# Whole float32 operands in place of split float32r ones in a two-layer transformer block

## What is computed

```
def layer1(x, Wq, Wk, Wv, Wo):                      # 16 heads of 128
    q, k, v = split_heads(x @ Wq), split_heads(x @ Wk), split_heads(x @ Wv)
    scores = einsum('bhsd,bhtd->bhst', q, k) * 128 ** -0.5 + mask   # 64-token blocks, |bi - bj| <= 2
    return merge_heads(einsum('bhst,bhtd->bhsd', softmax(scores), v)) @ Wo

def layer2(x, w_router, wq, bq, wk, bk, wv, bv, wo, w_gate, w_up, w_down, ln1_w, ln2_w):
    sel, sel_scores, pos = the 128 tokens of each batch with the highest x . w_router
    h = rms_norm(sel, ln1_w)
    q, k, v = rope(h @ wq + bq), rope(h @ wk + bk), h @ wv + bv     # 16, 8 and 8 heads of 128
    x1 = sel + merge(causal_attention(q, k, v)) @ wo                # all 256 rows one sequence
    h2 = rms_norm(x1, ln2_w)
    processed = x1 + (silu(h2 @ w_gate) * (h2 @ w_up)) @ w_down     # 2048 wide
    g = sigmoid(sel_scores)
    return x with the chosen rows set to g * processed + (1 - g) * sel

x = layernorm(x + layer1(x, ...))
x = layernorm(x + layer2(x, ...))
```

## Time and profile before

| | |
|---|---|
| runs | 1374.06, 1374.06, 1374.99 us; median 1374.06 |
| profiled execution | 1373.61 us, its span 1371.9 us |
| mean granted TensorE clock | 0.981 |
| busy: TensorE matmul / VectorE / ScalarE / GpSimd | 94% / 58% / 44% / 18% |
| HBM | 79.20 MB read, 8.91 MB written |

### The profile page before, as it was taken

How to read it: one execution, slowest core, us unless ns; L and a number is a source line. 1 busy time by engine, 2 the same in 40 slices (tenths; PEclk the granted TensorE clock), 3 DMA queues, 4 the chain that set the end, 5 groups by cost and what they waited for, 6 DMA issues and landing times.

```text
span 1371.9 us, 19013 instructions
## 1 busy us (share of the span) xinstructions
PE 1290.8 (94%) x7296; PEld 1097.2 (80%) x7296; DVE 791.8 (58%) x2219; ACT 605.3 (44%) x1422; POOL 247.6 (18%) x234
## 2 busy tenths in 40 slices
PE   6999999999999999988999999999999948999897
PEld 5888989898989898877798979898989834445696
DVE  4556565556565656566666756655565657542244
ACT  4544444454444444444454434354444433334353
POOL 2111111111111201023120212020211121000086
PEclk9999999999999999999999999999999979999898
DMA  5110100010111102022310101010101035555063
GB/s 167 41 32 16 47 30 33 32 32 31 32 32 47 62 1 77 1 100 70 123 47 16 47 27 47 16 47 16 47 16 46 24 137 188 192 194 169 0 192 131
DMA packets 62411, 89.34 MB, mean 65 GB/s; under 512 B 3232, under 2 KB 36000, under 8 KB 62320
## 3 DMA queue, kind: packets, MB, share of 16 engines
q1 hardware_dynamic: 61904, 86.81, 19.3%
q0 software_dynamic: 416, 1.31, 0.3%
HBM read 79.20 MB, written 8.91 MB: 64 GB/s over the span
## 4 chain that ended last, share of the span: by engine, by line
PE 75%; DVE 13%; ACT 6%; issue 2%; DMA 2%; POOL 2%; SPq 0%; ACTq 0%; POOLq 0%; DVEq 0%
PE proj L872 34%; PE y L872 11%; PE s L872 8%; PE o L872 8%; DVE arena L1343 6%; PE tp L951 4%; PE proj L880 3%; PE s L880 3%; ACT arena L1142 3%; ACT prob L1180 2%; DVE prob L1378 1%; PE o L880 1%; DVE bn_out L1442 1%; POOL arena L1651 1%; DVE yacc L1428 1%
## 5 line engine op out<-in xcount | busy, mean ns | idle before, releaser
L872 PE MATMUL proj<-arena 128*128 128x256 f32 (+1 forms) x3456 | 633.6, 333 | 8.5 <-DVE arena L1343 8.2
L872 PEld LDWEIGHTS proj<-arena 128*128 128x128 f32 x3456 | 531.2, 190 | 72.0 <-DVE arena L1343 13.1
L1180 ACT ACTIVATE prob<-prob,stat 128x384 f32<-128x384 f32 (+1 forms) x256 | 150.9, 590 | 488.7 <-DVE stat L1378 488.7
L1651 POOL TENSOR_TENSOR arena<-wraw,arena 128x1024 fp32r<-128x1024 f32 x75 | 182.1, 2438 | 861.7 <-ACT arena L1142 861.6
L1343 DVE TENSOR_TENSOR arena<-proj,arena 128x512 fp32r<-128x512 f32 (+1 forms) x266 | 148.0, 562 | 305.4 <-ACT arena L1142 304.3
L872 PE MATMUL s<-arena 128*128 128x384 f32 (+2 forms) x870 | 194.0, 336 | 11.1 <-DVE arena L1343 11.1
L872 PE MATMUL y<-arena 128*128 128x512 f32 x762 | 199.2, 397 | 0.5 <-DVE yacc L1428 0.5
L872 PE MATMUL o<-arena 128*128 128x256 f32 (+2 forms) x960 | 197.0, 325 | 0.7 <-DVE arena L1343 0.6
L1343 DVE TENSOR_TENSOR arena<-tp,arena 128x384 fp32r<-128x384 f32 (+2 forms) x257 | 133.6, 520 | 82.1 <-ACT arena L1142 81.8
L872 PEld LDWEIGHTS s<-arena 128*128 128x128 f32 x870 | 150.3, 189 | 29.9 <-DVE arena L1343 16.3
L1142 ACT ACTIVATE arena<-proj 128x512 fp32r<-128x512 f32 (+1 forms) x266 | 127.9, 488 | 95.1 <-PE proj L872 87.5
(11 more groups left out here) (151 smaller groups left out, 692.3 us busy)
## 6 DMA issues: line engine op xcount, KB each, us to landing
wraw<-in_L_attn_Wq SPq DMA_DIRECT2D x16, 512.0 KB, 3.4
wraw<-in_L_attn_Wk SPq DMA_DIRECT2D x16, 512.0 KB, 3.3
wraw<-in_L_attn_Wv SPq DMA_DIRECT2D x16, 512.0 KB, 3.3
wraw<-in_L_attn_Wo SPq DMA_DIRECT2D x16, 512.0 KB, 3.7
late<-in_L_ffn_wq SPq DMA_DIRECT2D x16, 512.0 KB, 4.9
late<-in_L_ffn_wo SPq DMA_DIRECT2D x16, 512.0 KB, 3.9
yacc<-in_L_attn_hidden_states SPq DMA_DIRECT2D x16, 256.0 KB, 3.0
y_dram<-yacc SPq DMA_DIRECT2D x16, 256.0 KB, 3.1
```

What stands on the lines that cost most here:

```text
L872: ins = e.matmul(out_ap, l[a], r[b], start=first and i == 0 and j == 0, stop=final and i == n - 1 and j == 2, skip_group_check=skip)
L1180: e.activation(prob[s][:, 0:n], prob[s][:, 0:n], ACT.Exp, bias=stat[:, 4 * s + 1:4 * s + 2], scale=-1.0, accum_out=stat[:, 4 * s + 2:4 * s ...
L1651: e.tensor_tensor(lo, wraw[n % RAW_SLOTS][:], hi.bitcast(F32), ALU.subtract).then_inc(*G_.inc("wsplit", n, "lo"))
```

## The change

All products take whole float32 operands, through one function. `hi_part`, `lo_part`, the weight splits, the raw places and `unit_row` go; ScalarE copies results out of PSUM once, and TensorE waits for that copy. The arena is one float32 tensor: both batches' turned x, q and k for two heads, v for two pairs of heads, four places for heads' outputs, and fifteen places for weights, through which all of `stream` passes, layer 2's attention weights included; a load is issued as its place is left. Batch 1's x is turned inside batch 0's heads (a tile every eighth unit), batch 0's by VectorE and ScalarE in turn. The bias and norm rows are loaded at the start into tiles of their own, and batch 0's routed rows are prepared from unit END - 8 on. In the MLP, VectorE writes the product straight into `aT`.

The diff, cut to its core:

```
-SPLIT_SLOTS, RAW_SLOTS = 5, 3
-O_SLOTS = 3
+PLACES = 15
+O_SLOTS = 4
...
-        sizes = dict(xT=2 * XT_N, q=2 * QK_N, k=2 * QK_N, v=2 * V_N, pT=2 * PT_N, oT=2 * O_SLOTS * O_N,
-                     w=2 * SPLIT_SLOTS * PIECE)
+        sizes = dict(xT=NB * XT_N, qk=4 * QK_N, v=2 * V_N, pT=PT_N, oT=O_SLOTS * O_N, w=PLACES * PIECE)
...
+        xT = [carve(start["xT"] + b * XT_N, KT, T) for b in range(NB)]
+        qT = [carve(start["qk"] + i * QK_N, T) for i in range(2)]
+        kT = [carve(start["qk"] + (2 + i) * QK_N, T) for i in range(2)]
+        vv = [carve(start["v"] + i * V_N, TT, GW) for i in range(2)]
+        pT = carve(start["pT"], PT_N)
+        oT = [carve(start["oT"] + s * O_N, T) for s in range(O_SLOTS)]
+        weight = [carve(start["w"] + i * PIECE, PIECE) for i in range(PLACES)]
...
+        hT = [carve(start["v"] + 3 * D, KT, P), carve(start["oT"], KT, P)]
...
+            n = len(place_of)
+            if n < len(stream) and free_places:
+                place_of[n], left_by[n] = free_places.pop(0)
+                landed[place_of[n]].plan(n)
...
+        def retire(key, *made):
+            free_places.append((place_of[number[key]], made))
             load_next()
...
-            need(which, b, h // HG)
-            hold("proj0", ("qk", H, which, c), V_, "qk", H, which, c, "lo")
+            hold("proj0", ("qk", H, which, c), S_, "qk", H, which, c, "copy")
...
+        bias_loaded.plan()
+        for who in (1, 2):
+            ln_loaded.plan(who)
...
         job("const")
-        lo_engine[0] = lambda n: "V"
         for t in range(4):
             load_resid(0, t)
         load_next()
         for t in range(4, TT):
             load_resid(0, t)
-        job("router")
+        load_next()
+        load_next()
+        job("rows1")
+        while free_places:
+            load_next()
...
+            turn_x(0, t, to, "VS"[t % 2])
...
+            t = u // TT - 5
+            if 0 <= t < TT:
+                if i == 0:
+                    load_x(1, t)
+                if i == 6:
+                    turn_x(1, t, "proj1" if r < 12 else "y", "S")
+            tick()
...
+            if u == END - 8:
                 begin(routed_in(0))
...
-        def three_passes(e, out_ap, pairs, first, final, skip=False):
-            n = len(pairs)
-            for i, (l, r) in enumerate(pairs):
-                for j, (a, b) in enumerate(((0, 0), (0, 1), (1, 0))):
-                    ins = e.matmul(out_ap, l[a], r[b], start=first and i == 0 and j == 0,
-                                   stop=final and i == n - 1 and j == 2, skip_group_check=skip)
-            return ins
-        def one_pass(e, out_ap, pairs, first, final, skip=False):
+        def product(e, out_ap, pairs, first, final, skip=False):
...
+                        for t in range(4 * c, 4 * c + 4):
+                            pe.wait_ge(*turned_at(b, t))
                         pe.wait_ge(*freed("proj0", "qk", H, which, c))
-                        three_passes(e, bank["proj0"][:, :], pairs[:KT // 2], True, False)
...
+                        pe.wait_ge(*bias_loaded.at())
                         row = BIAS_AT[which] + c
-                        ins = e.matmul(to, spread(unit_row[:, row:row + 1], P), ub, start=False, stop=True,
+                        ins = e.matmul(to, spread(ident[0:8, row:row + 1], P), bias[:, :], start=False, stop=True,
                                        skip_group_check=True)
...
-            def hi_part(dst, src, *name):
-                e.activation(dst, src, ACT.Copy).then_inc(*S_.inc(*name, "hi"))
-            def whole_copy(dst, src, *name):
+            def copy(dst, src, *name):
                 e.activation(dst, src, ACT.Copy).then_inc(*S_.inc(*name, "copy"))
...
+                    if H > 1:
                         done = {("q", 0): 3, ("q", 1): 7, ("k", 0): 4, ("k", 1): 7}[which, c]
-                        act.wait_ge(*T_.at("scores", H - 1, done, "made"))
...
+                    act.wait_ge(*(T_.at("out", NB * NG - 2, TT - 1, "made") if b else weighed(NHEADS - HG - 1, TT - 1)))
...
-            def lo_part(dst_lo, src, dst_hi, *name):
-                dve.wait_ge(*S_.at(*name, "hi"))
-                e.tensor_tensor(dst_lo, src, dst_hi.bitcast(F32), ALU.subtract).then_inc(*V_.inc(*name, "lo"))
...
+                    dve.wait_ge(*T_.at(kind, b, t, "made"))
+                    e.tensor_copy(xT[b][:, :, t * P:(t + 1) * P],
+                                  bank[bank_of["turn", b, t]][:, :].rearrange("p (k n) -> p k n", k=KT)
+                                  ).then_inc(*V_.inc(kind, b, t, "copy"))
...
+                    e.tensor_tensor(aT[ft % A_SLOTS], work[f][:, 0:NT], bank[f"proj{f}"][:, NT:2 * NT], ALU.mult
...
-                if kind == "wsplit" and key[1] == "G":
-                    n = key[0]
-                    hi, lo = wsp[slot_of[n]]
-                    pool.wait_ge(*S_.at("wsplit", n, "hi"))
-                    e.tensor_tensor(lo, wraw[n % RAW_SLOTS][:], hi.bitcast(F32), ALU.subtract
-                                    ).then_inc(*G_.inc("wsplit", n, "lo"))
...
+                if kind == "rows1":
                     e.dma_start(router[:], on_all_rows(w_router, 0, D)).then_inc(router_loaded.sem, 16)
+                    e.dma_start(ln1_row[:], on_all_rows(ln1_w, 0, D)).then_inc(ln_loaded.sem, 16)
+                    e.dma_start(ln2_row[:], on_all_rows(ln2_w, 0, D)).then_inc(ln_loaded.sem, 16)
+                    e.dma_start(bias[:], bqkv.rearrange("(n d) -> n d", n=8)).then_inc(bias_loaded.sem, 16)
...
-                    if n >= RAW_SLOTS:
-                        m = n - RAW_SLOTS
-                        sp.wait_ge(*(G_ if split_on[m] == "G" else V_).at("wsplit", m, "lo"))
+                    if left_by[n] is not None:
+                        sp.wait_ge(*T_.at(*left_by[n]))
                     src = stream[n][1]
-                    e.dma_start(wraw[n % RAW_SLOTS][:].rearrange("p (k n) -> p k n", k=src.shape[1]), src
-                                ).then_inc(raw_loaded[n % RAW_SLOTS].sem, 16)
+                    e.dma_start(weight[place_of[n]].rearrange("p (k n) -> p k n", k=src.shape[1]), src
```

More of the change, by code:

```diff
@@ L191, in build @@
[L191 to L212, removed]
@@ L365, in build, with wide @@
         stream.append((("o", NB - 1, NG - 1), rows(Wo, NG - 1)))
+        def wide(w, c, half):
+            return w[half * GW:(half + 1) * GW, c * 512:(c + 1) * 512].rearrange("(k p) n -> p k n", p=P)
+        for b in range(NB):
+            for n, (which, c) in enumerate(QKV_ORDER):
+                stream += [(("p2", b, n, half), wide(dict(q=wq, k=wk, v=wv)[which], c, half)) for half in range(2)]
+            stream += [(("o2", b, c), rows(wo, c)) for c in range(NH * HD // GW)]
         for c in range(FF // GW):
@@ L371, in build @@
         number = {key: n for n, (key, _) in enumerate(stream)}
-        def wide(w, c, half):
-            return w[half * GW:(half + 1) * GW, c * 512:(c + 1) * 512].rearrange("(k p) n -> p k n", p=P)
-        def pieces2(b):
-            found = []
-            for n, (which, c) in enumerate(QKV_ORDER):
-                found += [(("p2", b, n, half), wide(dict(q=wq, k=wk, v=wv)[which], c, half)) for half in range(2)]
-            return found, [(("o2", b, c), rows(wo, c)) for c in range(NH * HD // GW)]
@@ L456, in project_v @@
             b, g = divmod(G, NG)
-            need("v", b, g)
-            hold("proj1", ("v", G, t), V_, "v", G, t, "lo")
+            hold("proj1", ("v", G, t), S_, "v", G, t, "copy")
             job("v", G, t)
@@ L468, in turn_probs @@
         def turn_probs(H, i):
-            hold("tp", ("tp", H, i), V_, "tp", H, i, "lo")
+            hold("tp", ("tp", H, i), S_, "tp", H, i, "copy")
             job("tp", H, i)
@@ L660, in residual2 @@
             yield "resh"
-            hold("o0", ("resh", b), V_, "resh", b, "lo")
+            hold("o0", ("resh", b), S_, "resh", b, "copy")
             job("resh", b)
         def gate_up(c):
-            need("g2", 0, c)
-            need("u2", 0, c)
             for f in range(2):
@@ L972, in tensor_program @@
                         closes = (half == 0 and j == 4) or (half == 1 and j == TT - 1)
-                        ins = three_passes(e, bank[f"o{half}"][:, c:c + n],
-                                           [(v_, [pT[z][:, at:at + n] for z in range(2)])], opens, closes, skip=True)
+                        ins = product(e, bank[f"o{half}"][:, c:c + n], [(v_, pT[:, at:at + n])], opens, closes, skip=True)
                     ins.then_inc(*T_.inc("pv", H, j, "made"))
@@ L1198, in scalar_program @@
                     act.wait_ge(*weighed(H, 4 if half == 0 else TT - 1))
[L1199 removed]
+                    copy(oT[H % O_SLOTS][:, half * CH:(half + 1) * CH], bank[f"o{half}"][:, :], "o", H, half)
                 elif kind == "ot":
```

441 lines of the change are left out of this document (129 added, 312 removed).

## The result

The changed kernel takes 1543.53 us (median of 4 runs, 1541.0 to 1546.38) against 1374.06: 1.1237 times as long, 95% interval 1.1213 to 1.126. The forecast was 1560, in a range of 1530 to 1590.

The account below looks back on a forecast made before the run. TensorE, its matmuls busy for 94% of the span, was taken as the bound. Profiled 1373.6 us + 206.2 (layer 1) + 14.9 (MLP) + 7 (bias) - 16 - 18 - 4 - 4 (given back) = 1560, range 1530 to 1590.

Parts of the forecast that it names:

- Prices of a product: Layer 1 on TensorE: 512 columns go from 0.695 to 0.86 us a product; all widths together add 206.2 us.
- The second rival: Layer 1 and MLP: a whole product pays four passes for three, 0.93 us for 512 columns; 1687 us, chance 0.03.
- Third rival: Layer 1 and MLP: a product is two records, each costing what a float32r record does, 0.232; 984 us, chance 0.02.
- MLP: The MLP's 128 products of 256 columns and 32 of 512 cost TensorE 14.9 us more.
- Bias: The 16 bias products go from 0.42 to 0.86 us each, +7 us; bounds 0 and +20.
- The wait for the routed rows, -16: TensorE's 16.8 us wait for batch 0's routed rows goes with earlier loads and step: -16 us, bounds -10 and -17.
- Gaps of steady layer 1, -18: Layer 1: TensorE's waits for low parts go, other waits stay; 18 us given back, bounds 0 and -24.
- Layer 2's attention, -4: 19.6 of 175 us idle there, mostly latency that stays; VectorE is freer: -4 us, bounds 0 and -8.
- Start, -4: First scores come earlier, with one weight piece ahead and the turning shared: -4 us, bounds 0 and -7.
- First rival: New waits, such as ScalarE's copies, replace the old; only the routed wait goes: 1586 us, chance 0.08.
- Queues: Weight loads on SyncE: layer 2's 72 pieces need 200 us against 212 of TensorE work, so no wait expected.
- The signs named: Right: a pair 79 us, TensorE 96%, MLP 82 to 85, VectorE under 480. Wrong: pair over 81 or under 77.

Follow-up runs that it names:

- the run of the bias: The changed kernel with the bias tile and unit column over all 128 partitions, zeros below row 8, in place of 8: 1537.5 us, ratio 1.1186.
- the second routed-rows run: Kernel before, bias and norm rows loaded at END - 24, batch 0's routed rows read three units earlier, one weight piece ahead of x at start: 1361.3 us.
- the third: Kernel before, as the second routed-rows run, plus VectorE's product of the routed rows one unit before TensorE's transposes of it: 1356.2 us, ratio 0.9884.

## Why the prediction was right

- **Prices of a product**: right to the hundredth. All were read from layer 2's whole products in the trace of before, and the 384 by a line between two widths. The pair of heads is 78.8 us, forecast 79. The second rival (0.93 for 512 columns) and the third (0.46) are out: the chain has 0.86.
- **MLP**: +15.7, forecast +14.9. The clock is low at its first products in both kernels and costs much the same there (32 products of 256 take 13.46 us where the old prices give 11.4, and 16.07 where the new ones give 13.8), so that is not the difference; 0.8 is within the rounding of the prices.
- **Bias**: forecast 0.86 a product, measured 1.05; +10 in place of +7. The row of 0.42 in the trace of before, nearly twice what other float32r records of 512 take (0.232), had said that a product of fewer rows has a cost of its own, and I bounded it without using it.
- **The wait for the routed rows, -16**: right in size (16.8 to 1.5). The reason, the bias's steps and load ahead of it on VectorE, is shown by the runs in part: the early rows alone took it to 7.8 in the kernel before, and late rows brought back only 3.1 of the wait in the changed one. The clock after the wait was not priced: in the kernel before it is 0.67 from 1116.4 to 1120.6, an estimate of 1.5 us more.
- **Gaps of steady layer 1, -18**: this is the term that was mis-sized, and beyond its own bounds of 0 and -24. Layer 1 gave back 52 us, 15 of them at the routed rows, so 36 or 37 in place of 18. The direct measure is the run with low parts of one column and whole products: 36 in the old layout, with the routed wait still there. The mechanism was the forecast's, the loss behind VectorE's low parts; its size was not. That 1543.5 still fell into 1530 to 1590 is owed to a range made from other errors as well. I had counted weight loads per 66 us, which found 27 us lost between 25 and 1090 us, and then kept nine of them for waits that I thought would stay; and I counted none of the loss of the last units, from 1090 to 1144 us, beyond the routed wait. Of 1118.9 us of layer 1 before, 1056 were sixteen pairs of 66.0, which leaves 62.9; of 1273.1 after, 1260.8 are sixteen of 78.8, which leaves 12.3. The difference, 50.6, is nearly the whole of the 52, so what came back lies in what layer 1 took over sixteen steady pairs.
- **Layer 2's attention, -4**: the stage grew by 6.7, of which the bias is 10, so it gave back 3.3. The half clock early in it (the run of the bias) shows that this figure can be some 5 us off in one execution.
- **Start, -4**: -2.2.
- **First rival**, nothing given back: out, since TensorE waits 3.9 us in the whole kernel for ScalarE's copies (3.2 in the banks s and proj, 0.7 in o).
- **Queues**: no weight DMA is waited for in the changed kernel, as said; but with six places one is, so my sum of bytes and work was not what made it safe.
- **Third rival and the records**: 512 columns at 2.4 GHz are 0.213 us, and each of a product's two records takes 0.43. So the half rate that the third rival was built on is the rate of a record, of which a product has two; it never spoke for 0.46 a product.
- **The signs named**: TensorE's share is 98% where I had said up to 96, and the MLP's 85.2 us and VectorE's 490 us busy lie just outside 82 to 85 and under 480. None of the signs of being wrong came.

## What to carry to other kernels

Where one engine is the bound, price an edit by the chain's rows of the same operation elsewhere in the same trace, at every width that it will have; that gave the time to 1.1%, and the change of 169.5 us to a tenth. What an edit on the other engines gives back is not the sum of the waits in the list: cut the span at steady periods (here 66.0 us a pair) and subtract, and ask of the rest what it holds, since losses also lie in the busy time. A wait can cost more than its length, since the granted clock can fall after it (3.1 us of wait, 5.5 of layer 1, in the run with late rows). Whole float32 products are 24% dearer here than three float32r passes at 512 columns, 22% at 384 and 21% at 256, so splitting pays wherever the splitting engines have room, and what they cost then is worth a run of its own.

## What the runs showed of the hardware

- A float32r pass of 512 columns costs 0.232 us in a dense stream (six in 1.39), a whole product 0.86, which is four times 0.215. 512 columns at 2.4 GHz are 0.213. So a float32r pass, with a weight load for each, has some 9% over it, and a whole product, with two weight loads, 1% over four times the columns. By these figures four against three come out as 1.24, not 1.33. What the 9% is was not tried.
- A product of 8 rows between products of 128 costs 0.19 us more, about as long as its weight load's record (183 ns): 1.05 with 8 rows, 0.86 with 128. Whether it is the small number or the change of number was not tried.
- After a wait of 4.6 us (late rows, at 1267.19) and one of 3.12 (the changed kernel, at 1302.66) TensorE's granted clock was 0.51, the level of 1.2 GHz; after one of 3.13 in the run of the bias it was 1.00. So a wait of that length can bring the clock down, and need not.
- VectorE's product of the routed rows (two operands in SBUF, 128x512) took 2.84 us in the kernel before and 2.25 in the second routed-rows run, each time while GpSimd subtracted weights, and 0.75 in the third, where GpSimd stood still. In the kernel before it took 0.73 for batch 1, where GpSimd stood still too. In order of time, the kernel before, then the third:

```profile
1113.44 5.11 POOL L1651 TENSOR_TENSOR arena<-wraw,arena 128x1024 fp32r<-128x1024 f32 x2
1113.50 2.84 DVE L1520 SCALAR_TENSOR_TENSOR works<-x_sel,gate,works 128x512 f32<-128x512 f32 x1 [0.50 <-POOL gate L1626]
1204.40 0.73 DVE L1520 SCALAR_TENSOR_TENSOR works<-x_sel,gate,works 128x512 f32<-128x512 f32 x1
```
```profile
1093.39 0.08 DVE L1388 DVE_READ_ACCUMULATOR2_ANT stat<- 128x1 f32 x1
1093.39 0.75 DVE L1532 SCALAR_TENSOR_TENSOR works<-x_sel,gate,works 128x512 f32<-128x512 f32 x1
```

The Trainium skill (GPSIMD Engine Reference, Specifications) says that GpSimd's SBUF interfaces are shared with VectorE, with contention where VectorE's instruction has two SBUF inputs, and (SBUF — State Buffer, Terms) that the loser waits for the whole instruction of the other. These rows agree: GpSimd's instruction lasts about 2.6 us (5.11 for two), and VectorE's 0.75 grew by 1.5 and 2.1. No run took GpSimd's instruction away at that place and left the rest, so this is read from the traces, not shown by an undoing.
